# Feed forward with Hadamard steps: rounding and subtraction moved from VectorE to ScalarE, in an order of stages written out

## The reference, cut to what matters

```python
def act_quant(x, bits=8):                 # per token
    qb = 128.0
    scale = qb / clip(max(abs(x), axis=-1), 1e-5)
    xq = clip(round(x * scale), -qb, qb - 1) / scale
    return xq
def bitlinear(x, w):   return act_quant(x) @ weight_quant(w).T
def h_bitlinear(x, w): return act_quant(fwht(x)) @ weight_quant(w).T   # fwht: normalized Hadamard transform
x = layernorm(x + ffn(x)),  where
ffn(x): h_bitlinear(silu(bitlinear(x, w_gate)) * bitlinear(x, w_up), w_down)
```

## Time and profile before

| | |
|---|---|
| median of 3 runs | 6014.61 us (6013.51 to 6016.92) |
| profiled execution | 6023.15 us, its span 6021.8 us |
| busy in the span | PE 4680.2 us (78%), DVE 3349.2 (56%), POOL 1794.8 (30%), ACT 1542.7 (26%) |

### The profile page before, as it was taken

The page is one execution under the profiler, slowest core; times in us unless marked ns, Lnnn a source line. Parts: engine busy times, 40 slices in busy tenths (PEclk is TensorE's granted clock), DMA queues, the critical chain, the costliest instruction groups (busy, mean ns, idle before and its releaser), DMA issues. The chain is left out here.

```text
span 6021.8 us, 62767 instructions
## 1 busy us (share of the span) xinstructions
PE 4680.2 (78%) x22022; PEld 2480.6 (41%) x22022; DVE 3349.2 (56%) x5407; ACT 1542.7 (26%) x2993; POOL 1794.8 (30%) x1747
## 2 busy tenths in 40 slices
PE   6997888899965743278799889824999995996487
PEld 4664222344432632145333333322555552442276
DVE  4554777667749986899544445451333334355622
ACT  1111676411111100244222222201211210443132
POOL 0002222001126667134201111146555553011311
PEclk9997999999975556688899999957999997996598
DMA  2000000100000002200000000024999985001000
GB/s 74 1 1 8 2 1 2 67 0 0 0 9 0 1 0 28 92 15 1 20 1 13 7 1 8 1 93 113 229 239 233 218 193 148 1 1 67 2 1 28
DMA packets 127015, 288.74 MB, mean 48 GB/s; under 512 B 22113, under 2 KB 25825, under 8 KB 124258
## 3 DMA queue, kind: packets, MB, share of 16 engines
q1 hardware_dynamic: 79826, 184.42, 9.5%
q0 software_dynamic: 46880, 100.30, 8.5%
HBM read 345.47 MB, written 67.96 MB: 69 GB/s over the span
## 5 line engine op out<-in xcount | busy, mean ns | idle before, releaser
L204 PE MATMUL ps<-arena 128*128 128x512 f32 (+18 forms) x17578 | 4096.8, 473 | 709.9 <-DMA arena<-in_L_gamma 82.3
L204 PEld LDWEIGHTS ps<-arena 128*128 128x128 f32 (+6 forms) x17578 | 1918.5, 170 | 2674.8 <-issue 1446.3
L209 PE MATMUL ps<-arena 128*128 128x128 f32 (+2 forms) x3420 | 460.3, 278 | 579.6 <-DMA arena<-moe_x,arena 154.6
L209 PEld LDWEIGHTS ps<-arena 128*128 128x128 f32 (+2 forms) x3420 | 382.8, 144 | 764.2 <-issue 481.6
L253 POOL TENSOR_SCALAR arena<-arena 128x1 f32<-128x1 f32 x192 | 74.3, 387 | 1589.4 <-DVE arena L247 1589.1
L2559 DVE SCALAR_TENSOR_TENSOR arena<-ps,arena 128x128 f32<-128x128 f32 x382 | 103.7, 313 | 534.3 <-ACT arena L2443 534.3
L2618 POOL DMA_INDIRECT moe_y<-arena x191 | 306.5, 1605 | 301.8 <-DVE arena L2576 241.8
L2004 DVE TENSOR_REDUCE arena<-ps 128x2 f32<-128x256 f32 (+3 forms) x256 | 199.2, 821 | 332.5 <-PE ps L204 332.5
L800 DVE TENSOR_REDUCE arena<-ps 128x2 f32<-128x1024 f32 x256 | 304.0, 1219 | 82.6 <-PE ps L204 81.8
L774 ACT ACTIVATE arena<-ps 128x512 f32<-128x512 f32 x512 | 277.6, 597 | 126.6 <-PE ps L204 124.0
L1983 ACT ACTIVATE arena<-ps 128x1024 f32<-128x1024 f32 (+3 forms) x256 | 166.2, 701 | 542.1 <-PE ps L204 542.1
(11 more groups left out here) (299 smaller groups left out, 4180.6 us busy)
## 6 DMA issues: line engine op xcount, KB each, us to landing
arena<-in_L_ffn_gu SPq DMA_DIRECT2D x191, 768.0 KB
arena<-in_L_ffn_dn SPq DMA_DIRECT2D x191, 256.0 KB
arena<-in_L_ffn_dn SPq DMA_DIRECT2D x191, 128.0 KB, 3.7
moe_y<-arena SPq DMA_DIRECT2D x8, 1024.0 KB
arena<-moe_y SPq DMA_DIRECT2D x8, 1024.0 KB
arena<-in_L_ffn_w SPq DMA_DIRECT2D x8, 1024.0 KB
arena<-in_x SPq DMA_DIRECT2D x4, 1024.0 KB
arena<-in_L_attn_W_qkvu SPq DMA_DIRECT2D x4, 1024.0 KB
```

The lines of the kernel that those rows point to most:

```text
L204: return self.nc.tensor.matmul(out, lhsT, rhs, start=start, stop=stop, skip_group_check=True)
L209: return self.nc.tensor.transpose(out, in_, ident[0:n, 0:n])
```

## The change

Scaling and rounding of the Hadamard result move to ScalarE: one activation computes HA * scale + MAGIC (Identity, with the scale and the bias read per partition). VectorE then bounds it in one pass, between MAGIC - 128 and MAGIC + 127. ScalarE subtracts MAGIC into YB. In the quantization of X the last of the three passes, the subtraction into XB, moves to ScalarE as well. GpSimd writes the constants MAGIC and -MAGIC once. The order of steps is no longer `skew` but a list: within one t, down of t-5, stats of t-4, hadamard of t-3, scale and clip of t-4, up of t-2, turn of t-1, quant of t. TensorE's and GpSimd's order of work is as before.

```diff
-    LAGS = (0, 1, 2, 3, 4, 5)
+    def order():
+        for t in range(NT + 5):
+            for what, lag in (("down", 5), ("stats", 4), ("hadamard", 3), ("scale", 4), ("clip", 4), ("up", 2), ("turn", 1), ("quant", 0)):
+                if 0 <= t - lag < NT:
+                    yield what, t - lag
...
     def scalar():
...
+            elif what == "scale":
+                act.wait_ge(dve, "hscale", i)
+                act.wait_ge(pool, "magic")
+                nc.scalar.activation(HA[i % 2], HA[i % 2], ACT.Identity, bias=MG[:, 0:1], scale=m[:, 5:6]).then_inc(
+                    *act.done("rounded", i))
+            elif what == "clip":
+                act.wait_ge(dve, "clip", i)
+                act.wait_ge(pe, "yt", i - 2, 1) if i >= 2 else None
+                nc.scalar.activation(YB[i % 2], HA[i % 2], ACT.Identity, bias=MG[:, 1:2]).then_inc(*act.done("yb", i))
+            elif what == "quant":
+                act.wait_ge(dve, "xq", i)
+                act.wait_ge(pe, "xt", i - 2)
+                act.wait_ge(pool, "magic")
+                nc.scalar.activation(XB[i % 2], XQ[i % 2], ACT.Identity, bias=MG[:, 1:2]).then_inc(*act.done("xb", i))
...
     def vector():
...
+                dve.wait_ge(act, "xb", i - 2)
                 nc.vector.tensor_scalar(XQ[i % 2], k.X[:, i, :], m[:, 1:2], 127.0, ALU.mult, ALU.min).then_inc(*dve.done())
                 dve.settle()
-                nc.vector.tensor_scalar(XQ[i % 2], XQ[i % 2], -128.0, MAGIC, ALU.max, ALU.add).then_inc(*dve.done())
-                dve.settle()
-                dve.wait_ge(pe, "xt", i - 2)
-                nc.vector.tensor_scalar(XB[i % 2], XQ[i % 2], MAGIC, None, ALU.subtract).then_inc(*dve.done("xb", i))
+                nc.vector.tensor_scalar(XQ[i % 2], XQ[i % 2], -128.0, MAGIC, ALU.max, ALU.add).then_inc(*dve.done("xq", i))
...
-                dve.wait_ge(dve, "hscale", i)
-                nc.vector.tensor_scalar(ha, ha, m[:, 5:6], 127.0, ALU.mult, ALU.min).then_inc(*dve.done())
-                dve.settle()
-                nc.vector.tensor_scalar(ha, ha, -128.0, MAGIC, ALU.max, ALU.add).then_inc(*dve.done())
-                dve.settle()
-                dve.wait_ge(pe, "yt", i - 2, 1) if i >= 2 else None
-                nc.vector.tensor_scalar(YB[i % 2], ha, MAGIC, None, ALU.subtract).then_inc(*dve.done("yb", i))
+            elif what == "clip":
+                ha = HA[i % 2]
+                dve.wait_ge(act, "rounded", i)
+                nc.vector.tensor_scalar(ha, ha, MAGIC - 128.0, MAGIC + 127.0, ALU.max, ALU.min).then_inc(*dve.done("clip", i))
```

More of the change, by code:

```diff
@@ L1584, in l1_ffn @@
     sm = k.alloc([NT, 12])
+    MG = k.alloc([2])
     early = k.W - 4104
@@ L1601, in tensor @@
     def tensor():
-        for s, i in skew(NT, LAGS):
-            if s == 1:
+        for what, i in order():
+            if what == "turn":
                 bb = eighths(R.take("xt", i, by=((act, "xt", i),)))
-                pe.wait_ge(dve, "xb", i)
+                pe.wait_ge(act, "xb", i)
                 for kk in range(4):
@@ L1608, in tensor @@
                 t.then_inc(*pe.done("xt", i))
-            elif s == 2:
+            elif what == "up":
                 pe.wait_ge(act, "xt", i)
@@ L1616, in tensor @@
                         t.then_inc(*pe.done(name, i, c))
-            elif s == 3:
+            elif what == "hadamard":
                 pe.wait_ge(dve, "u", i, 3)
@@ L1629, in tensor @@
                     t.then_inc(*pe.done("ha", i, c))
-            elif s == 5:
-                pe.wait_ge(dve, "yb", i)
+            elif what == "down":
+                pe.wait_ge(act, "yb", i)
                 for c in range(2):
@@ L1643, in scalar @@
     def scalar():
-        for s, i in skew(NT, LAGS):
-            if s == 1:
+        for what, i in order():
+            m = sm[:, i, :]
+            if what == "turn":
                 act.wait_ge(pe, "xt", i)
@@ L1662, in scalar @@
                     act.wait_ge(pe, "ha", i, c)
-                    act.wait_ge(dve, "yb", i - 2)
+                    act.wait_ge(act, "yb", i - 2)
                     nc.scalar.activation(HA[i % 2][:, 512 * c:512 * c + 512], R.of("ha", i, c), ACT.Copy).then_inc(
                         *act.done("ha", i, c))
-            elif s == 5:
+            elif what == "scale":
[12 more added lines that the diff above has]
+                nc.scalar.activation(XB[i % 2], XQ[i % 2], ACT.Identity, bias=MG[:, 1:2]).then_inc(*act.done("xb", i))
+            elif what == "down":
                 for c in range(2):
@@ L1673, in vector @@
     def vector():
-        for s, i in skew(NT, LAGS):
+        for what, i in order():
             m = sm[:, i, :]
-            if s == 0:
+            if what == "quant":
                 nc.vector.tensor_reduce(m[:, 0:1], k.X[:, i, :], AX.X, ALU.max, apply_absolute_value=True).then_inc(*dve.done())
@@ L1706, in vector @@
                 butterfly(nc.vector.tensor_tensor, i, 1, ALU.subtract).then_inc(*dve.done("b1", i))
-            elif s == 4:
+            elif what == "stats":
                 ha = HA[i % 2]
@@ L1735, in gpsimd @@
     def gpsimd():
-        for s, i in skew(NT, LAGS):
-            if s == 3:
+        nc.gpsimd.memset(MG[:, 0:1], MAGIC).then_inc(*pool.done("magic+"))
+        nc.gpsimd.memset(MG[:, 1:2], -MAGIC).then_inc(*pool.done("magic"))
+        for what, i in order():
+            if what == "hadamard":
                 pool.wait_ge(dve, "b1", i)
```

## The result

The changed kernel takes 6090.81 us (median of 3 runs, 6086.24 to 6091.06) for 6014.61: the ratio is 1.0124, with a 95% interval of 1.0101 to 1.0147, 76.2 us slower. The forecast was 6090. The profiled execution takes 6091.06 us, its span 6089.8. Its stage, from the first maximum of |X| (L1699) at 2559.40 to the last sum at 3030.98, takes 471.6 us; before it was 397.8 (2564.8 to 2962.65). That is 73.8 us more.

A forecast was written before the change was run, and what follows sets the result against it. VectorE's row, busy 230.42 of 235.24 us, was taken as the bound. Rounds of 11.2 + 7.55 + 10.62 = 29.37 us for 23.5 gave +75.6 us in all, forecast 6090 us by the median, range 6050 to 6125.

The forecast's parts named there:

- E = T0 + 11.2: In an inner round, XQ ends (E) 11.2 us after VectorE ends its four butterflies (T0); 10.08 with the third pass.
- S = E + 7.55: VectorE's next sum (S) starts 7.55 us after XQ ends, behind XB subtraction, YT copies and down product.
- 5.65 us for the product: TensorE's 16 matmuls of the down step, ahead of the sum, take 5.65 us, bounds 5.3 and 6.5.
- T0 = S + 10.62: VectorE ends the next butterflies 10.62 us after the sum starts: last HA copy at 5.92, then 4.67.
- The sum: Whole stage, tile by tile: rounds of 29.37 us for 23.5, in all +75.6 us.
- First sum: The stage's first sum on VectorE, before at 2622.42, comes 5.7 us later, at 2628.15.
- Eleven rounds: The eleven rounds after the stage's first sum take 323.1 us for 258.26, +64.8.
- The last four distances: Between the stage's last sums: 24.0, 23.4, 21.5 and 18.2 us, changes of +1.1, +2.0, +4.7 and -2.7.
- Rival 1: VectorE's shorter row counts: inner rounds of 21.0 us, 2.5 us less, 5985 us; chance 5%.
- Rival 2: Same chain, but TensorE at full clock or XQ not held up by GpSimd: 6060 us; chance 14%.
- Rival 3: ScalarE reloads its function table between Silu and Identity, 15 to 31 us more: 6105 to 6121; chance 8%.
- Rival 4: No change in time: the chain takes just what VectorE saves; chance 2%.

The follow-up runs named there:

- e9_silu_only: Changed kernel with ScalarE's four Silus ahead of the YB subtraction, the XB subtraction left ahead of the YT copies; 6064.87 us, ratio 1.0083.
- e1_xb_late: Changed kernel with only ScalarE's XB subtraction moved behind the YT copies of the next round; ratio 1.0004.
- e3_xb_only: Kernel before with only the XB subtraction moved to ScalarE, at the end of its round; ratio 1.0114.
- e4_filled: Changed kernel with twelve more matmuls a tile on TensorE just ahead of the down product; ratio 1.0098.
- e7_before_reordered: Kernel before, its passes still on VectorE, with the steps reordered and a PSUM bank for the down product alone; ratio 0.9971.
- e8_no_queueing: Changed kernel with steps reordered, a PSUM bank for the down product, XB subtraction behind ScalarE's IT, HA and YT copies; 5956.3 us, ratio 0.9904.
- e2_xb_vector: Changed kernel with the XB subtraction put back on VectorE behind XQ; ratio 0.9987.

## Why the prediction was right

- **E = T0 + 11.2.** Measured 10.92 (2751.22 to 2762.14). Bounding came in ahead of GpSimd, whose four steps stretched from 9.64 to 10.48 us behind it. By the Trainium skill (SBUF — State Buffer, Who interferes with whom) the shared port pair goes to whoever comes first; the trace agrees, bounding starting at 2751.22 and GpSimd at 2751.38. The first Silu kept VectorE idle for 2.71 us, forecast 2.7. That this wait counts, and isn't swallowed by GpSimd's last step, e9_silu_only showed: without it XQ ends a step earlier.
- **S = E + 7.55.** Measured 8.04 and 6.91 in turn (2762.14 to 2770.18, 2791.73 to 2798.64), mean 7.5. No single round had the forecast's 5.65 us for the product: from its start to the sum it was 6.22 and 5.10 in turn, and that the mean is 5.66 is luck, since the value was taken between two rows and what sets it wasn't found out. That the place of the XB subtraction makes this term is shown from both sides: moved out of the way alone (e1_xb_late) the round loses it, moved in alone (e3_xb_only) the kernel before gets it.
- **T0 = S + 10.62.** Measured 10.62 (2770.18 to 2780.80), with 0.74 us of wait for the last HA copy, forecast 0.8.
- **The sum.** First sum: forecast +5.7, measured 64.8 us from the first L1699 for 57.6, +7.2; the Hadamard products of the second tile also ran slower, with gaps of 0.70 and 0.90 us between the HA copies for 0.30. Eleven rounds: +64.8, measured 320.1 for 258.3, +61.8. The last four distances: +1.1, +2.0, +4.7, -2.7; measured 23.93, 23.65, 21.52 and 17.61 us, +1.0, +2.2, +4.7, -3.2. In all +75.6, measured +73.8. That the whole time came out within 1 us of the forecast is luck in part: outside this stage the profiled execution of the changed kernel takes 5618.2 us for 5624.0 of before, and before's execution lay 8.5 us above its median, the changed kernel's 0.25.
- **Rivals.** Rival 1 fell: VectorE's row did become shorter, 175 us for 230 in some ten rounds, but the round became longer. Rival 2 fell: 6.19 us and 5.06 us in turn is not the full clock, which e4_filled shows at 3.6, and XQ was held up by GpSimd, its last pass taking 2.44 us. Rival 3 fell, as Identity beside Silu brought no load and the way from S to T0 didn't grow. Rival 4 fell with the 1.24%. There is one table load in the whole stage:

```profile
L1663 ACT ACT_TABLE_LOAD  x1: 1283/1283/1283, 2564.7 to 2564.7; - x1
```

By the Trainium skill (ScalarE: Activation LUTs, Rules for kernel authors) multiplications and additions belong on VectorE. Pass by pass the trace agrees: 2.00 and 2.08 us on ScalarE, 1.22 us on VectorE. But e7_before_reordered and e8_no_queueing show that here the longer passes on the engine with room win 0.67%, once they stand in the right place.

## What to carry to other kernels

An instruction that waits late holds back everything behind it in its engine's program: before moving work to an engine that has room, look at what stands behind the new instruction and who waits for that. Here one pass of 0.72 us, put ahead of two copies, cost 5 us a round, more than all that the move saved. Behind those copies it no longer held them up (e1_xb_late), and in the order of e8_no_queueing it waited for nothing itself. When busy time falls and the time rises, follow the wait of the engine that used to be the bound back through the others until it comes to that engine again.

## What was not expected of the hardware

The same product of 16 matmuls took 6.19 us (clock 0.57) and 5.06 us (0.71) in successive rounds of the changed kernel, 6.1 us in the rounds of e1_xb_late that were read (0.58), and 4.17 us (0.86), 5.14 (0.69) and 5.59 (0.64) in e2_xb_vector, although TensorE's pauses ahead of it were alike in the last two: 2.32, 0.46 and 1.1 us in one, 2.32, 0.46 and 0.5 to 1.3 in the other. What decides it wasn't found out; it is most of the 1.2 us a round between those two runs. Twelve matmuls in the pause brought it to 3.6 us at a clock of 1.00 in eight rounds of eleven, and in e8_no_queueing, where TensorE is busy for 92%, the clock was 1.00 all along.
